# Mamba phase: state sums by accumulating float32 transposes, gate by token

## The reference

```python
xz = x @ W_in.T
xp, z = jnp.split(xz, 2, axis=-1)
xc = silu(conv1d_causal_4_taps(xp) + conv_b)
proj = xc @ W_xproj.T
dt, Bt, Ct = jnp.split(proj, [12, 28], axis=-1)
dt = softplus(dt @ W_dt.T + b_dt)
def step(h, inp):
    dA = jnp.exp(dt_t[..., None] * A)
    h = dA * h + (dt_t * x_t)[..., None] * B_t[:, None, :]
    y = jnp.einsum('bdn,bn->bd', h, C_t)
...
y = ys + xc * D_param
y = y * silu(z)
return y @ W_out.T
...
return 0.5 * (y_fwd + y_bwd)
```

## Time and profile before

| | us |
|---|---|
| median of 3 runs | 4730.69 |
| lowest and highest run | 4727.85, 4736.11 |
| span of the profiled execution (first to last instruction) | 4718.1 |

### The profile page before, as it was taken

The page is one execution under the profiler, slowest core; times in us unless marked ns, Lnnn a source line. Parts: engine busy times, 40 slices in busy tenths (PEclk is TensorE's granted clock), DMA queues, the critical chain, the costliest instruction groups (busy, mean ns, idle before and its releaser), DMA issues. The chain is left out here.

```text
span 4718.1 us, 62490 instructions
## 1 busy us (share of the span) xinstructions
PE 4271.6 (91%) x16896; PEld 2235.4 (47%) x16896; DVE 3251.1 (69%) x5016; ACT 2430.7 (52%) x4880; POOL 3212.3 (68%) x1669
## 2 busy tenths in 40 slices
PE   7999986997899999999999999999999876999994
PEld 4666644664343443344334434433443334666673
DVE  5667773111699999999999999989999975111114
ACT  3555542122566666767676666667666633222221
POOL 3222222442799999999999999999999941444441
PEclk9999996998899999999999999999999987999997
DMA  1000011342334333334333333333333321333456
GB/s 35 21 20 20 20 53 59 108 127 76 107 114 125 115 118 116 121 109 121 122 112 115 112 121 118 116 118 113 117 107 123 114 67 45 110 116 112 127 169 219
DMA packets 267113, 478.79 MB, mean 101 GB/s; under 512 B 39404, under 2 KB 176444, under 8 KB 266908
## 3 DMA queue, kind: packets, MB, share of 16 engines
q1 hardware_dynamic: 235776, 403.02, 26.9%
q0 software_dynamic: 28032, 73.17, 6.1%
q10 hardware_dynamic: 3100, 0.64, 0.1%
HBM read 409.75 MB, written 41.81 MB: 96 GB/s over the span
## 5 line engine op out<-in xcount | busy, mean ns | idle before, releaser
L1804 POOL TENSOR_TENSOR m_xh<-m_u,m_Bb 128x1536 f32<-128x1536 f32 x512 | 1780.1, 3550 | 51.6 <-DVE m_u L1675 39.0
L1731 PE MATMUL bank<-m_xh,ident 128*128 128x512 f32 x3072 | 1455.1, 609 | 34.3 <-POOL m_xh L1793 34.3
L1773 DVE TENSOR_TENSOR_SCAN bank<-bank,m_xh 128x512 f32<-128x512 f32 x864 | 1038.9, 1216 | 44.5 <-ACT bank L1760 42.2
L1760 ACT ACTIVATE bank<-m_dt,m_Ac 128x508 f32<-128x508 f32 x1536 | 1024.9, 683 | 38.4 <-DVE m_xh L1773 38.4
L1731 PEld LDWEIGHTS bank<-m_xh,ident 128*128 128x128 f32 x3072 | 576.2, 194 | 820.0 <-issue 730.7
L1773 DVE TENSOR_TENSOR_SCAN m_xh<-bank,m_xh 128x512 f32<-128x512 f32 x672 | 787.8, 1207 | 64.8 <-ACT bank L1760 59.3
L1793 POOL TENSOR_TENSOR m_xh<-m_xh,m_Cb 128x1536 f32<-128x1536 f32 x224 | 794.0, 3544 | 4.3 <-DVE m_xh L1773 4.0
L1784 DVE TENSOR_TENSOR m_xh<-bank,m_Cb 128x512 f32<-128x512 f32 x864 | 581.3, 673 | 10.9 <-DMA m_Cb<-BC_rows 10.8
L1204 ACT ACTIVATE f1t_h<-bank,f1t_b 128x512 f32<-128x512 f32 (+1 forms) x276 | 147.6, 586 | 509.9 <-PE bank L1234 509.9
L1134 POOL DMA_INDIRECT rows_y<-f1t_y,f1t_home x142 | 139.9, 985 | 316.4 <-DVE f1t_y L1175 287.1
L1579 PE MATMUL bank<-m_xp,m_dg 128*128 128x512 f32 x768 | 351.9, 601 | 3.7 <-DVE m_u L1675 1.4
(11 more groups left out here) (367 smaller groups left out, 6148.3 us busy)
## 6 DMA issues: line engine op xcount, KB each, us to landing
m_Bb<-BC_rows SPq DMA_DIRECT2D x256, 512.0 KB, 4.8
m_Cb<-BC_rows SPq DMA_DIRECT2D x256, 512.0 KB, 4.0
f1t_w<-f_w SPq DMA_DIRECT2D x46, 576.0 KB
m_r<-m_dt POOLq DMA_DIRECT2D x32, 768.0 KB, 7.4
f1t_w1a<-f_w SPq DMA_DIRECT2D x46, 384.0 KB
f0t_w<-f_w SPq DMA_DIRECT2D x22, 576.0 KB
f1c_yg<-rows_y SPq DMA_DIRECT2D x16, 768.0 KB, 8.3
f1t_w1b<-f_w SPq DMA_DIRECT2D x92, 96.0 KB
```

Source lines behind the costliest of these rows:

```text
L1731: mm = pe.matmul(bank[:, c, :], K.ident[:, :], xh[n % NX][:, c, :], start=False, stop=(d == 1 and n == NS - 1))
L1760: act.activation(o[:, :, lo:hi], seqs(dt[d][:, c, :])[:, :, lo:hi], ACT.Exp, scale=Ac[:, c, n:n + 1]).then_inc(s_dA, 1)
L1773: dve.tensor_tensor_scan(o, bank[:, RING[d][p], way], xh[n % NX][:, c, way], 0.0, ALU.mult, ALU.add).then_inc(s_h, 1)
L1804: pool.tensor_tensor(xh[n % NX][:, :, :], u[d][:, :, :], Bb[q % RB][:, n % QN, :].unsqueeze(1).to_broadcast([P, DC, TOK]), ALU.mult).then_ ...
```

## The change

Sums: `pe_sum` no longer streams 512 columns of `h*C` through the identity. For each of the 4 sequences it takes the 128 x 128 block of `h*C` as the stationary operand and transposes it (`is_transpose=True`) onto the accumulating bank. The sums then stand with tokens on the partitions and channels along the free side. `pe_D` is turned the same way (4 matmuls of 128 columns), and so is `pe_gate` (8 matmuls of 128 columns), so that the gate is by token too. `dve_y` multiplies as before, into `ysT`, which is the buffer `gz`.

The gated rows must be turned back for the output projection. A new PE step `pe_yT` (4 transposes for each chunk) and a new ACT step `act_yT` (a copy for each chunk to `ys`, now the buffer `lw`) do this. `pe_D` of the next group waits for that copy instead of for `dve_y`.

The positions move: the D terms of slot 0 from 14, 15, 17 to 17, 18, 20; the output projection from 17, 18 to 20, 21; `dve_out` from 14, 15 to 16, 17; `pe_dt` of slot 0 from 20, 21, 22 to 13, 17, 19 with its ACT steps from 19, 21, 22 to 14, 16, 18; `act_pj` of slot 0 from 10 to 11. `pe_out` now waits until the last `act_abs` of the slot has read bank 7, where before `pe_dt` waited for the output projection.

```diff
--- before.py
+++ after.py
@@ -1365,12 +1365,13 @@
         NQ, QN = 8, 2
         UNITS = NS * DC
         POS = {
-            "y": (6, 7, 9), "pe_D0": (14, 15, 17), "pe_D1": (6, 16, 25), "pe_out": (17, 18), "out": (14, 15),
+            "y": (6, 7, 9), "pe_yT": (15, 16, 18), "act_yT": (12, 13, 15), "pe_D0": (17, 18, 20), "pe_D1": (6, 16, 25), "pe_out": (20, 21),
+            "out": (16, 17),
             "act_rows": (11, 13), "rows": (12, 14), "stats": 14, "rstd": 18, "norm": 40,
             "pe_zT": (43, 46), "act_zT": (44, 45), "pe_x0": (0, 1, 2), "act_x0": (0, 1, 4), "pe_conv0": (3, 4, 5),
-            "act_conv0": (6, 10, 12), "pe_conv1": (0, 2, 4), "act_conv1": (1, 4, 7), "pe_gate1": (23, 26, 31), "act_gate1": (25, 27, 30),
-            "pe_dt0": (12, 14, 16), "act_dt0": (17, 20, 22), "pe_dt1": (20, 21, 22), "act_dt1": (19, 21, 22), "pe_pj": (10, 11),
-            "act_pj": (15, 10), "act_xc": (14, 8), "act_e": (23, 23), "act_w1": (23, 26), "act_ln": (26, 29),
+            "act_conv0": (6, 10, 12), "pe_conv1": (0, 2, 4), "act_conv1": (1, 4, 7), "pe_gate1": (25, 27, 31), "act_gate1": (25, 27, 30),
+            "pe_dt0": (12, 14, 16), "act_dt0": (17, 20, 22), "pe_dt1": (13, 17, 19), "act_dt1": (14, 16, 18), "pe_pj": (10, 11),
+            "act_pj": (15, 11), "act_xc": (14, 8), "act_e": (23, 23), "act_w1": (23, 26), "act_ln": (26, 29),
             "pe_sp0": (26, 36, 40), "act_sp0": (30, 39, 41), "u0": (34, 38, 41), "pe_sp1": (32, 38, 42), "act_sp1": (34, 38, 40),
             "u1": (32, 37, 40),
         }
@@ -1407,12 +1408,12 @@
         z = sb("z", [P, G, C])
         xc = [sb(f"xc{d}", [P, DC, TOK]) for d in two]
         r = sb("r", [P, DC, TOK])
-        ys = r
         dt = [sb(f"dt{d}", [P, DC, TOK]) for d in two]
         u = [sb(f"u{d}", [P, DC, TOK]) for d in two]
         e, w1 = dt, u
         lw = sb("lw", [P, DC, TOK])
         gz = sb("gz", [P, DC, TOK])
+        ysT, ys = gz, lw
         RB, RC = 4, 2
         Bb = [sb(f"Bb{b}", [P, QN, TOK]) for b in range(RB)]
         Cb = [sb(f"Cb{b}", [P, QN, TOK]) for b in range(RC)]
@@ -1433,6 +1434,7 @@
         s_copied = sem("rows_in_psum")
         s_er, = ctx.software(K, 1)
         s_gy, s_ops, s_out = sem("gated_ready"), sem("outps_ready"), sem("res_ready")
+        s_yTps, s_yT = sem("gatedT_ready"), sem("gatedT_copied")
 
         def seqs(t):
             return t.rearrange("p (b t) -> p b t", b=G)
@@ -1555,16 +1557,24 @@
             def pe_gate(pe, c):
                 if c == 0:
                     pe.wait_ge(s_abs, (s + 1) * 2 * DC)
+                    if deep:
+                        stand_alone(pe, K.go)
+                        pe.wait_ge(s_out, g * 2)
                 else:
                     pe.wait_ge(s_zc, g * DC + c)
                 m = slice((DC + c) * P, (DC + c + 1) * P)
-                pe.matmul(bank[:, front(c), :], win_a[:, m], zTa[:, :], start=True, stop=False)
-                pe.matmul(bank[:, front(c), :], win_b[:, m], zTb, start=False, stop=True).then_inc(s_zps, 1)
+                for j in range(G):
+                    t = slice(j * P, (j + 1) * P)
+                    pe.matmul(bank[:, front(c), t], zTa[:, t], win_a[:, m], start=(j == 0), stop=False)
+                for j in range(G):
+                    t = slice(j * P, (j + 1) * P)
+                    mm = pe.matmul(bank[:, front(c), t], zTb[:, t], win_b[:, m], start=False, stop=(j == G - 1))
+                mm.then_inc(s_zps, 1)
 
             def act_gate(act, c):
                 act.wait_ge(s_zps, g * DC + c + 1)
                 if c == 0 and deep:
-                    act.wait_ge(s_gy, g * DC)
+                    act.wait_ge(s_yTps, g * DC)
                 act.copy(gz[:, c, :], bank[:, front(c), :]).then_inc(s_zc, 1)
 
             def pe_conv(pe, c):
@@ -1609,9 +1619,6 @@
             def pe_dt(pe, c):
                 if c == 0:
                     pe.wait_ge(s_pj, s + 1)
-                    if d == 1 and deep:
-                        stand_alone(pe, K.go)
-                        pe.wait_ge(s_out, g * 2)
                 elif not first:
                     pe.wait_ge(s_abs, s * 2 * DC + 2 * c)
                 pe.matmul(bank[:, front(c), :], wdt[:, c * P:(c + 1) * P], low[PD:PD + R, :], start=True, stop=True).then_inc(s_dtps, 1)
@@ -1622,8 +1629,6 @@
                     act.wait_ge(s_spps, s * DC)
                     if deep:
                         act.wait_ge(s_dA, (s - 1) * UNITS)
-                    if d == 1 and deep:
-                        act.wait_ge(s_ops, g * 2)
                 act.activation(e[d][:, c, :], bank[:, front(c), :], ACT.Abs, bias=bdt[:, c:c + 1]).then_inc(s_abs, 1)
                 act.activation(r[:, c, :], bank[:, front(c), :], ACT.Relu, bias=bdt[:, c:c + 1]).then_inc(s_abs, 1)
 
@@ -1641,6 +1646,8 @@
                 act.wait_ge(s_w1, s + 1)
                 if not first:
                     act.wait_ge(s_spps, s * DC)
+                    if d == 1 and deep:
+                        act.wait_ge(s_ops, g * 2)
                 act.activation(lw[:, :, :], w1[d][:, :, :], ACT.Ln).then_inc(s_ln, 1)
                 act.wait_ge(s_ln, s + 1)
                 act.activation(w1[d][:, :, :], w1[d][:, :, :], ACT.Identity, bias=K.ones[:, 0:1], scale=-1.0).then_inc(s_nc, 1)
@@ -1718,24 +1725,44 @@
         def pe_D(pe, g, d, c):
             pe.wait_ge(s_xc, g * 2 + d + 1)
             if d == 0 and later(g):
-                pe.wait_ge(s_gy, (g - 1) * DC + c + 1)
+                pe.wait_ge(s_yT, (g - 1) * DC + c + 1)
             elif d == 0:
                 pe.wait_ge(s_u, DC)
-            pe.matmul(bank[:, c, :], dgD[:, c, :], xc[d][:, c, :], start=(d == 0), stop=False).then_inc(s_D, 1)
+            for j in range(G):
+                t = slice(j * P, (j + 1) * P)
+                mm = pe.matmul(bank[:, c, t], xc[d][:, c, t], dgD[:, c, :], start=(d == 0 and j == 0), stop=False)
+            mm.then_inc(s_D, 1)
 
         def pe_sum(pe, g, d, n, c):
             if n not in BY_POOL[d]:
                 pe.wait_ge(s_prv, dve_reads(g, d, n) + c + 1)
             elif c == 0:
                 pe.wait_ge(s_prp, pool_reads(g, d, n + 1))
-            mm = pe.matmul(bank[:, c, :], K.ident[:, :], xh[n % NX][:, c, :], start=False, stop=(d == 1 and n == NS - 1))
+            for j in range(G):
+                t = slice(j * P, (j + 1) * P)
+                mm = pe.matmul(bank[:, c, t], xh[n % NX][:, c, t], K.ident[:, :], is_transpose=True, start=False,
+                               stop=(d == 1 and n == NS - 1 and j == G - 1))
             mm.then_inc(s_red, 1)
+
+        def pe_yT(pe, g, c):
+            pe.wait_ge(s_gy, g * DC + c + 1)
+            for j in range(G):
+                t = slice(j * P, (j + 1) * P)
+                mm = pe.transpose(bank[:, c, t], ysT[:, c, t], K.ident[:, :])
+            mm.then_inc(s_yTps, 1)
+
+        def act_yT(act, g, c):
+            act.wait_ge(s_yTps, g * DC + c + 1)
+            if c == 0 and not (isinstance(g, int) and g == NG - 1):
+                act.wait_ge(s_spps, (g * 2 + 3) * DC)
+            act.copy(ys[:, c, :], bank[:, c, :]).then_inc(s_yT, 1)
 
         def pe_out(pe, g, i):
             if i == 0:
-                pe.wait_ge(s_gy, g * DC + DC)
+                pe.wait_ge(s_yT, g * DC + DC)
                 if not (isinstance(g, int) and g == NG - 1):
-                    pe.wait_ge(s_pj, g * 2 + 4)
+                    stand_alone(pe, K.go)
+                    pe.wait_ge(s_abs, (g * 2 + 4) * 2 * DC)
             else:
                 pe.wait_ge(s_out, g * 2 + 1)
             for j in (2 * i, 2 * i + 1):
@@ -1808,7 +1835,7 @@
             dve.wait_ge(s_red, (g * 2 * NS + 2 * NS - 1) * DC + c + 1)
             if c == 0:
                 dve.wait_ge(s_gz, g + 1)
-            dve.tensor_tensor(ys[:, c, :], bank[:, c, :], gz[:, c, :], ALU.mult).then_inc(s_gy, 1)
+            dve.tensor_tensor(ysT[:, c, :], bank[:, c, :], gz[:, c, :], ALU.mult).then_inc(s_gy, 1)
 
         def dve_out(dve, g, i):
             dve.wait_ge(s_ops, g * 2 + i + 1)
@@ -1899,6 +1926,8 @@
             def _(pe):
                 def main(pe, g, d, p, end):
                     carry = d == 0 and later(g)
+                    if carry and p in POS["pe_yT"]:
+                        pe_yT(pe, g - 1, POS["pe_yT"].index(p))
                     if carry and p in POS["pe_D0"]:
                         pe_D(pe, g, d, POS["pe_D0"].index(p))
                     at_D = POS["pe_D1"] if later(g, d) else (1, 4, 7)
@@ -1914,6 +1943,8 @@
                     for n in range(NS - LAG, NS):
                         for c in range(DC):
                             pe_sum(pe, NG - 1, 1, n, c)
+                    for c in range(DC):
+                        pe_yT(pe, NG - 1, c)
                     for i in two:
                         pe_out(pe, NG - 1, i)
                 program(pe, "pe", main, lambda pe: None, after)
@@ -1922,7 +1953,13 @@
             def _(act):
                 def main(act, g, d, p, end):
```

(8 more changed lines are left out.)

## The result

| kernel | median, us | ratio to before, 95% interval |
|---|---|---|
| before | 4729.27 | |
| after | 4883.15 | 1.0329 [1.0315, 1.0342] |

What follows compares the result with a forecast made beforehand. POOL's own work was taken as the floor, 160.5 us a group. Half B +4.2, clock +1.7, half A -1.9 gave +4.0 us a group; 15 groups +60, group 0 -2: 4789 us, range 4700 to 4855.

Steps and rivals of the forecast that it cites:

- the clock's term: Slot 0's serial chain: PE's 4.1 us gap before `act_abs` 0 brings half clock, costing 1.7 us a group.
- half B: Part of a group from dBx at 2502.67 to 2584.77, 82.1 us; forecast 4.2 us longer before the clock's 1.7.
- half A: Part of a group from dBx at 2584.77 to 2665.83, 81.1 us; forecast 1.9 us shorter.
- The sums: PE's sums: four transposes cost 0.44 us instead of 0.86; PE falls from 96% to about 72% busy.
- Stalls that go: Waits removed: `dve_y` at position 6 gains 1.9 us, half A gains 1.9, waits at half B's `u` shrink.
- The walk of positions 11 to 18: Slot 0: PE, ACT and DVE form one serial chain; DVE is 7.7 us later at position 18.
- faster rival: Positions 11 to 18 overlap more; delay below 5.4 us shortens the group, below 2.8 gives 4689 us; chance 0.23.
- milder form: Sparse sums let PE's clock fall at several places, adding 2 to 4 us a group: 4820 to 4855; chance 0.11.
- What takes it up: Vanishing waits at `u` absorb 3.5 us of DVE's delay; the third `u` comes 4.2 us later.
- POOL at dBx 8: POOL waits 2.4 us for the third sum at position 20, inside the 4.2 us of half B.
- Two passes: Transposed sums run as two passes and stay at 0.86 us: about 4860 us; chance 0.02.
- Clock lost throughout: Transposes don't hold the clock, PE at 1.2 GHz through the phase: over 4930 us; chance 0.04.

Runs made afterwards that it cites:

- warm_everywhere: after, plus unused matmuls in slot 0's two idle stretches of PE and matmuls of zeros at sparse positions of both slots: 4790.63 us.
- fill_more: before with the transposed sums, D, gate and turning back in before's positions, plus matmuls of zeros where PE has little to do: 4691.73 us.
- warm_by_transposes: after, plus 40 unused transposes in slot 0's two idle stretches, behind the projection and the second `pe_yT`: 4883.25 us.
- output_later: after with `dve_out` moved to positions 19 and 22, the second `pe_out` to 23, and two `pe_gate` steps one position later: 4833.08 us.
- warm_by_matmuls: after, plus five unused matmuls of 512 columns in slot 0's two idle stretches, behind the projection and the second `pe_yT`: 4880.53 us.

## Why the prediction was right or wrong

The sign was right, and the time, 4789 us, was 94 us too low; after lies above the range (4855). Of the 94 us, 66 are the clock's term (91 measured, 25 forecast). The rest is the difference between warm_everywhere, 4791 us, and the 4764 that the sum gives without that term: half B grew by 5.3 us and not by 4.2, half A lost 1.0 and not 1.9. Step by step:

**The sums.** Right: four records, 20 of them in 2.35 us, a pitch of 0.11 us ((2.35 - 0.27)/19) at the full clock. PE's share in the 400 us was 79% instead of 72%: at the lower clock the same work lasts longer.

**Stalls that go.** Half right. `dve_y` waits 0.97 us instead of 2.10, not zero (0.04 on average in warm_everywhere, so this too is the clock). Half A was forecast at -1.9 us: it is -1.0 in warm_everywhere and -1.5 in fill_more, but +0.5 in after, where 17 of its 82 us are at the lower clock (before: 4).

**The walk of positions 11 to 18.** Right in its mechanism, and near in size where the clock is mostly kept. Scan 18 was to be 7.7 us late before the clock's share; in warm_everywhere it is 39.9 - 31.9 = 8.0. DVE's waits of "about 5" and 1.1 us are 5.17 and 1.30. Half B was to grow by 4.2, without the clock: 5.3 measured (87.1 against 81.8). That the delay agrees so well may be in part luck, since 10 us of this half B are still at 1.2 GHz. The faster rival's deciding number, a delay under 5.4 us, was not reached, and the order is what kept it from that: in fill_more, with the positions of before, there is no delay (31.6) and the time is 4691.73, beside the 4689 of POOL's floor.

**The clock: the step that failed.** This term of the sum had the right mechanism and was mis-sized. The forecast took one gap at half clock, 1.7 us a group, 25 us in all. From warm_everywhere to after it is 91 us, 6.1 a group: the delay at scan 18 is 13.2 instead of 8.0 us, half B 92.3 instead of 87.1, half A 81.6 instead of 80.1. Two things had been missed. First, in the chain the lower clock is not one short stretch behind one gap; it stands on both sides of it, 28.7 us in a half B. In the trace of after, from `pe_dt` 0 to `pe_dt` 1 it is 5.74 us (walk: 6.0); from 1 to 2 it is 8.23 (walk: 5.9), with `pe_dt`, D, a sum and `pe_yT` all at twice their length; from 2 to `pe_out` 4.39 (walk: 3.0). `pe_proj`, ahead of all that, takes 4.47 us instead of 2.77, behind a gap of 2.06 us. Secondly, the clock falls among the sparse sums too, where PE is idle for less than 2 us at a time, as at 2719.6; half A has no part in the chain, and 17.1 us of it are at 1.2 GHz. Its one long gap, 4.27 us before 2740.84, can't be all of that: before has it too (3.67 us before 2644.25), and 4 us of a half A at the lower clock. This was the rival's "milder form", given 0.11 and 2 to 4 us a group on top of the 1.7; measured were 6.1 - 1.7 = 4.4, just above its upper end. The row that I let decide, 525.3 to 528.7, has PE busy for 64% of the time. It answers whether transposes can hold the clock, and they can (warm_by_transposes). The question was whether a PE that is only partly busy keeps its clock, and for that I had no row at the density of the new sums, 0.44 us for each 1.7 us position, or 26%. I should have taken the milder form into the forecast.

**What takes it up.** The slack was forecast at 3.5 us and is 2.7: 8.0 us of delay became 5.3 in half B at the mostly kept clock, and 13.2 became 10.5 in after. The place was wrong: POOL was to wait 4 us or more at the third `u`, but from 1400 to 3600 us its waits for `u` come to 2.9 us in all. DVE's delay reaches it at a read, behind a scan (3.80 us at 2664.25).

**POOL at dBx 8.** 2.4 us forecast, 6.52 measured (6.4 on average). In warm_everywhere the average is 2.3, so it was right for the kept clock, and the clock's step made the miss. In output_later this wait, not DVE's, sets half B. The forecast held it to be inside DVE's delay; in after DVE's scan does end POOL's last long wait of the half, the read's.

**The other rivals.** Two passes: refuted by the records. Clock lost throughout: not so, 771 us of 2780 are at the lower level.

## What to carry to other kernels

When a change takes work off an engine that has a granted clock, price what is left of its work on the path at both clocks, and look at the granted clock in the stretches that get sparse, not just in those where it stands idle. If it turns sparse, a few matmuls of zeros in places that nobody waits for can be worth more than the work saved: here the change as made lost 154 us, and its first half with such fillers, in the old order, gained 34. Ahead of every sum, where others wait for what follows, the same filler cost 109 us.

## What was unexpected of the hardware

- The clock fell to 1.2 GHz without a long gap: in after it is at the lower level from 2719.6 to 2729.8 us, and the longest idle time of PE in the ten us before is 1.87 us.
- The clock makes the same instructions take different times. In after, half A alternates between 80.2 and 83.4 us from group to group, with 13.7 us at the lower level in the short ones and 20.5 or more in the long ones. A filler in slot 0 (warm_by_matmuls) changed this in half A, which follows it: all but one of its halves are long ones.
